# Grouped experts: gate and up products of the first 512 tokens moved into the router's stretch

## What is computed

```python
scores = jax.nn.sigmoid(h @ gate_w.T)                 # 32 experts
sc = scores + gate_bias
grp = sc.reshape(-1, G, E // G)                       # 8 groups of 4
gidx = top_k(top_k(grp, 2)[0].sum(-1), 4)[1]          # best 4 groups
masked = where(in_best_groups, sc, 0)
tki = top_k(masked, 8)[1]                             # best 8 experts
tkw = take(scores, tki); tkw = 2.5 * tkw / (tkw.sum(-1) + 1e-20)
combine = (one_hot(tki, E) * tkw[..., None]).sum(1)
g = silu(einsum('th,eih->tei', h, w_gate)); u = einsum('th,eih->tei', h, w_up)
routed = einsum('tei,ehi->th', g * u * combine[:, :, None], w_down)
shared = silu(h @ sh_gate.T) * (h @ sh_up.T) @ sh_down.T
x = x + layernorm(routed + shared)
```

## Time and profile before

| | |
|---|---|
| timed runs, median (lowest to highest) | 3097.4 us (3094.87 to 3097.8) |
| profiled execution, span | 3093.3 us |
| busy share: PE / DVE / ACT / POOL | 87% / 66% / 51% / 35% |
| last stage, first and last instruction of its engines | about 2849.7 to 3084.4 us |

### The profile page before, as it was taken

How to read it: one execution, slowest core, us unless ns; L and a number is a source line. 1 busy time by engine, 2 the same in 40 slices (tenths; PEclk the granted TensorE clock), 3 DMA queues, 4 the chain that set the end, 5 groups by cost and what they waited for, 6 DMA issues and landing times. The chain is left out here.

```text
span 3093.3 us, 55201 instructions
## 1 busy us (share of the span) xinstructions
PE 2694.2 (87%) x21256; PEld 1684.6 (54%) x21276; DVE 2049.2 (66%) x4308; ACT 1572.2 (51%) x3080; POOL 1072.5 (35%) x784
## 2 busy tenths in 40 slices
PE   8985899999799799999998888898877899777698
PEld 4552555566676566666666566465543334335465
DVE  5668999935644665546664665566439999996554
ACT  4334788852423444434554555366456676643122
POOL 3201000001243344434443553245226777773000
PEclk9995899989899899999999899998999999998899
DMA  1000000001120200000000000000013344340000
GB/s 55 1 4 1 2 3 3 3 2 82 33 89 22 84 1 1 1 1 1 1 1 1 29 1 1 1 1 1 1 66 129 137 144 144 136 143 21 1 1 14
DMA packets 34228, 105.41 MB, mean 34 GB/s; under 512 B 3456, under 2 KB 14592, under 8 KB 33200
## 3 DMA queue, kind: packets, MB, share of 16 engines
q1 hardware_dynamic: 31952, 97.69, 9.1%
q0 software_dynamic: 2016, 4.19, 0.4%
HBM read 94.01 MB, written 7.86 MB: 33 GB/s over the span
## 5 line engine op out<-in xcount | busy, mean ns | idle before, releaser
L2121 POOL TENSOR_TENSOR many_probs<-many_probs,many_rinv 128x2048 f32<-128x2048 f32 (+7 forms) x128 | 269.6, 2106 | 358.8 <-DVE many_rinv L2161 358.8
L1101 DVE TENSOR_REDUCE heads_halfmax<-heads_qmajor 128x1 f32<-128x512 f32 x512 | 316.3, 681 | 32.7 <-PE heads_qmajor L962 29.4
L3509 DVE TENSOR_TENSOR_SCAN stream_state<-stream_decay,stream_state 128x512 f32<-128x512 f32 x256 | 306.3, 1233 | 0.9 <-ACT stream_decay L3341 0.5
L1066 ACT ACTIVATE weights<-heads_kmajor 128x1024 f32<-128x1024 f32 x256 | 259.2, 1026 | 71.7 <-PE heads_kmajor L974 65.7
L2090 ACT ACTIVATE many_probs<-many_score,many_negmax 128x1024 f32<-128x1024 f32 (+7 forms) x256 | 187.4, 737 | 173.1 <-DVE many_negmax L2145 173.1
L2145 DVE TENSOR_REDUCE many_negmax<-many_score 128x1 f32<-128x1024 f32 (+7 forms) x256 | 184.4, 751 | 106.0 <-PE many_score L2019 104.3
L3179 PE MATMUL stream_yacc<-stream_state,ident 128*128 128x512 f32 x512 | 249.1, 614 | 0.4 <-POOL stream_state L3471 0.4
L3341 ACT ACTIVATE stream_decay<-weights,mamba_negA 128x512 f32<-128x512 f32 x256 | 173.0, 689 | 112.5 <-DVE stream_state L3509 111.3
L3471 POOL TENSOR_TENSOR stream_state<-XN,stream_state 128x1024 f32<-128x1024 f32 x85 | 200.2, 2359 | 81.6 <-DVE stream_state L3509 81.2
L2027 PE MATMUL many_ring<-ident,many_probs 128*128 128x128 f32 x1152 | 174.6, 279 | 23.4 <-POOL many_probs L2121 6.5
L3500 DVE TENSOR_TENSOR stream_state<-stream_bspread,stream_du 128x1024 f32<-128x1024 f32 x128 | 153.2, 1197 | 46.6 <-POOL stream_du L3447 38.6
(11 more groups left out here) (586 smaller groups left out, 5925.5 us busy)
## 6 DMA issues: line engine op xcount, KB each, us to landing
XN<-mamba_crows SPq DMA_DIRECT2D x85, 512.0 KB, 3.6
stream_crow<-mamba_crows SPq DMA_DIRECT2D x43, 512.0 KB, 3.7
weights<-in_w_dram SPq DMA_DIRECT2D x1, 6148.0 KB, 17.3
weights<-in_w_dram SPq DMA_DIRECT2D x1, 4274.0 KB, 12.9
weights<-in_w_dram SPq DMA_DIRECT2D x1, 3296.0 KB, 10.9
swiglu_pairs<-swiglu_fetched SPq DMA_DIRECT2D x1, 2310.0 KB, 10.4
weights<-in_w_dram SPq DMA_DIRECT2D x1, 2112.0 KB, 8.2
swiglu_fetched<-swiglu_pairs SPq DMA_DIRECT2D x4, 528.0 KB, 7.3
```

Of the source, the lines that this page charges most:

```text
L1066: nc.scalar.activation(probs_of(k).rearrange("p (a n) -> p a n", a=2), kmajor[:, at:at + 2, :], ACT.Exp, scale=SC).then_inc(exp_done, 1)
L1101: nc.vector.tensor_reduce(halfmax[:, g % 2, at, h % 2:h % 2 + 1], qmajor[:, (2 * n + j) % 3, :], AX, ALU.max).then_inc(max_done, 1)
L2121: nc.gpsimd.tensor_tensor(pair, pair, rinv[:, n % 4, :].unsqueeze(2).broadcast_to([P, 2, wide]), ALU.mult).then_inc(norm_done, 1)
L3509: nc.vector.tensor_tensor_scan(h[:, part(half)], decay[:, (2 * g + half) % DECAYS, :], h[:, part(half)], 0.0 if half == 0 else h[:, BANK - ...
```

## The change

Gate and up of the whole first block (`AHEAD` = 17 units) are issued on TensorE right after the router's matmuls, while VectorE runs the router. ScalarE takes the Silu of each into `ahead` and copies the up product from PSUM to `up_kept` (two buffers, so the copy waits for the product two units back). GpSimd multiplies the two in SBUF and leaves the result in `ahead`. The first half's transposes stand ahead of unit 15 on TensorE (`FIRST_TURN`), the second half's ahead of unit 16 (`SECOND_TURN`), and ScalarE's copies of them likewise. In the loop over all units TensorE then has only spread and down for units 0 to 16, and VectorE only the product with `spread`, with `ahead` as its second operand. From unit 17 on the loop is as before.

For the shared expert there is no spread any more. In the first block its down takes `ahead` directly, and in the others VectorE writes the product of up and Silu straight to `hidden`. So `wide_ones` is gone, and `hidden_at`, `unit_of`, `spread_at` and `unit_of_spread` turn unit numbers into counts of `hidden` and `spread` and back.

```diff
@@ -3570,6 +3570,20 @@
...
     UNITS = [(tc, c) for tc in range(NT // 4) for c in range(CH + 1)]
+    AHEAD = CH + 1
+    FIRST_TURN, SECOND_TURN = 15, 16
+
+    def hidden_at(n):
+        return n if n < CH else n - 1
+
+    def unit_of(h):
+        return h if h < CH else h + 1
+
+    def spread_at(n):
+        return n - n // (CH + 1)
+
+    def unit_of_spread(k):
+        return k + k // CH
     with Phase(nc, "grouped") as ph:
...
@@ -3586,8 +3600,9 @@
...
         select = ph.sb("select", [96, CH, P], BF16)
+        ahead = ph.sb("ahead", [P, AHEAD, BANK])
+        up_kept = ph.sb("up_kept", [P, 2, BANK])
         silu = ph.sb("silu", [P, 2, BANK])
-        wide_ones = ph.sb("wide_ones", [1, BANK])
         gated = ph.sb("gated", [P, 2, BANK])
...
@@ -3599,21 +3614,26 @@
...
                                 "sel_done"))
+        silu_ahead, up_ahead, ahead_done = ph.sem("silu_ahead"), ph.sem("up_ahead"), ph.sem("ahead_done")
         nz = Normaliser(nc, m, ph, "n_", True, False, EARLY[s])
...
         def _(pool):
-            nc.gpsimd.memset(wide_ones[:], 1.0).then_inc(sel_done, 1)
             nc.gpsimd.memset(select[:], 0.0).then_inc(sel_done, 1)
             for r in range(3):
-                pool.wait_ge(sel_done, r + 2)
+                pool.wait_ge(sel_done, r + 1)
 
...
                                         pattern=[[-2, CH], [-1, 2], [0, 64]], channel_multiplier=1).then_inc(sel_done, 1)
+            for n in range(AHEAD):
+                pool.wait_ge(silu_ahead, n + 1)
+                pool.wait_ge(up_ahead, n + 1)
+                nc.gpsimd.tensor_tensor(ahead[:, n, :], ahead[:, n, :], up_kept[:, n % 2, :],
+                                        ALU.mult).then_inc(ahead_done, 1)
             for q in EARLY[s]:
...
@@ -3628,45 +3648,57 @@
...
                 tc, c = UNITS[n]
-                if n >= 2:
-                    pe.wait_ge(gated_done, n - 1)
+                if 2 <= n < AHEAD + 2:
+                    pe.wait_ge(up_ahead, n - 1)
+                elif n >= AHEAD + 2:
+                    pe.wait_ge(gated_done, n - 1 - AHEAD)
                 for k in range(2):
...
                                      start=True, stop=True).then_inc(gu_done, 1)
-            gate_and_up(0)
-            gate_and_up(1)
-            pe.wait_ge(parts_done, 1)
-            for half in range(2):
-                if half:
-                    pe.wait_ge(turn_kept, 1)
+
+            def turn(half):
                 for j in range(8):
...
                 last.then_inc(turn_done, 1)
-            pe.wait_ge(turn_kept, 2)
-            pe.wait_ge(sel_done, 5)
+
+            for n in range(AHEAD):
+                if n == FIRST_TURN:
+                    pe.wait_ge(parts_done, 1)
+                    turn(0)
+                if n == SECOND_TURN:
+                    pe.wait_ge(turn_kept, 1)
+                    turn(1)
+                gate_and_up(n)
+            pe.wait_ge(sel_done, 4)
             for n in range(len(UNITS) + 1):
...
                     tc, c = UNITS[n]
-                    if n >= 2:
+                    if n >= AHEAD:
                         gate_and_up(n)
-                        pe.wait_ge(hid_done, n - 1)
                     if c < CH:
-                        nc.tensor.matmul(spread[:, n % 2, :], select[:, c, :], partsT[:, tc * BANK:(tc + 1) * BANK],
+                        if spread_at(n) >= 2:
+                            pe.wait_ge(hid_done, hidden_at(unit_of_spread(spread_at(n) - 2)) + 1)
+                        if c == 0 and tc == 2:
+                            pe.wait_ge(turn_kept, 2)
+                        nc.tensor.matmul(spread[:, spread_at(n) % 2, :], select[:, c, :],
+                                         partsT[:, tc * BANK:(tc + 1) * BANK],
                                          start=True, stop=True).then_inc(spread_done, 1)
-                    else:
-                        nc.tensor.matmul(spread[:, n % 2, :], m.ones[0:1, :], wide_ones[0:1, :], start=True,
-                                         stop=True).then_inc(spread_done, 1)
                 if n >= 1:
                     tc, c = UNITS[n - 1]
-                    pe.wait_ge(hid_done, n)
+                    if n - 1 == CH:
+                        pe.wait_ge(ahead_done, AHEAD)
+                        left = ahead[:, CH, :]
+                    else:
+                        pe.wait_ge(hid_done, hidden_at(n - 1) + 1)
+                        left = hidden[:, hidden_at(n - 1) % 3, :]
                     if c == 0 and tc > 0:
...
                         wt = shared_w[2] if c == CH else w["wd"][:, c * P:(c + 1) * P]
-                        last = nc.tensor.matmul(down[:, 0, j * P:(j + 1) * P], hidden[:, (n - 1) % 3, j * P:(j + 1) * P],
+                        last = nc.tensor.matmul(down[:, 0, j * P:(j + 1) * P], left[:, j * P:(j + 1) * P],
                                                 wt, start=(c == 0 and j == 0), stop=(c == CH), skip_group_check=True)
...
@@ -3674,16 +3706,28 @@
...
             nc.scalar.activation(scores[:].rearrange("p t e -> p (t e)"), spread[:, 0, :], ACT.Sigmoid).then_inc(sig_done, 1)
-            for half in range(2):
+            def keep_turn(half):
                 act.wait_ge(turn_done, half + 1)
...
                                      ACT.Copy).then_inc(turn_kept, 1)
-            for n in range(len(UNITS)):
+
+            for n in range(AHEAD):
+                if n == FIRST_TURN:
+                    keep_turn(0)
+                if n == SECOND_TURN:
+                    keep_turn(1)
                 act.wait_ge(gu_done, 2 * n + 1)
+                nc.scalar.activation(ahead[:, n, :], gate_up[:, 2 * (n % 2), :], ACT.Silu).then_inc(silu_ahead, 1)
+                act.wait_ge(gu_done, 2 * n + 2)
                 if n >= 2:
-                    act.wait_ge(gated_done, n - 1)
+                    act.wait_ge(ahead_done, n - 1)
+                nc.scalar.activation(up_kept[:, n % 2, :], gate_up[:, 2 * (n % 2) + 1, :], ACT.Copy).then_inc(up_ahead, 1)
+            for n in range(AHEAD, len(UNITS)):
+                act.wait_ge(gu_done, 2 * n + 1)
+                if n >= AHEAD + 2:
+                    act.wait_ge(gated_done, n - 1 - AHEAD)
                 nc.scalar.activation(silu[:, n % 2, :], gate_up[:, 2 * (n % 2), :], ACT.Silu).then_inc(silu_done, 1)
-                if UNITS[n][1] == 7 and UNITS[n][0] >= 1:
+                if UNITS[n][1] == 7:
                     nz.scale(act, 0, UNITS[n][0] - 1)
...
@@ -3741,16 +3785,30 @@
...
                 if n < len(UNITS):
-                    dve.wait_ge(silu_done, n + 1)
-                    dve.wait_ge(gu_done, 2 * n + 2)
-                    nc.vector.tensor_tensor(gated[:, n % 2, :], gate_up[:, 2 * (n % 2) + 1, :], silu[:, n % 2, :],
-                                            ALU.mult).then_inc(gated_done, 1)
-                    dve.wait_ge(gated_done, n + 1)
-                    dve.wait_ge(spread_done, n + 1)
-                    if n >= 3:
-                        dve.wait_ge(down_done, n - 2)
-                    nc.vector.tensor_tensor(hidden[:, n % 3, :], spread[:, n % 2, :], gated[:, n % 2, :],
-                                            ALU.mult).then_inc(hid_done, 1)
+                    h = hidden_at(n)
+                    shared = UNITS[n][1] == CH
+                    if n >= AHEAD:
+                        dve.wait_ge(silu_done, n + 1 - AHEAD)
+                        dve.wait_ge(gu_done, 2 * n + 2)
+                        if shared:
+                            dve.wait_ge(down_done, unit_of(h - 3) + 1)
+                        into = hidden[:, h % 3, :] if shared else gated[:, n % 2, :]
+                        product = nc.vector.tensor_tensor(into, gate_up[:, 2 * (n % 2) + 1, :], silu[:, n % 2, :], ALU.mult)
+                        product.then_inc(gated_done, 1)
+                        if shared:
+                            dve.wait_ge(gated_done, n + 1 - AHEAD)
+                            dve.sem_inc(hid_done, 1)
+                        else:
+                            dve.wait_ge(gated_done, n + 1 - AHEAD)
+                    elif not shared:
+                        dve.wait_ge(ahead_done, n + 1)
+                    if not shared:
+                        dve.wait_ge(spread_done, spread_at(n) + 1)
+                        if h >= 3:
+                            dve.wait_ge(down_done, unit_of(h - 3) + 1)
+                        left = ahead[:, n, :] if n < AHEAD else gated[:, n % 2, :]
+                        nc.vector.tensor_tensor(hidden[:, h % 3, :], spread[:, spread_at(n) % 2, :], left,
+                                                ALU.mult).then_inc(hid_done, 1)
                 if n >= 1 and UNITS[n - 1][1] == CH:
...
                     dve.wait_ge(down_done, n)
```

## The result

| | before | changed |
|---|---|---|
| median (lowest to highest) | 3097.6 us (3094.87 to 3099.36) | 3071.5 us (3070.43 to 3073.03) |
| profiled execution, span | 3093.3 us | 3068.7 us |
| first gate and up to the last copy of `Y` (VectorE) | 228.2 us | 203.7 us |
| first gate and up to unit 17's | 79.65 us | 58.68 us |

The ratio is 0.9913, 95% interval 0.9901 to 0.9925: 26.1 us less. 3077.0 was forecast, with 3064 to 3087 as the range. The forecast gain was 20.4 us, the spans differ by 24.6.

What follows compares the result with a forecast made beforehand. TensorE was taken as the bound in the loop, idle while VectorE ran the router. Gains of 17.3 us up to unit 17 and 3.15 from the ones make 20.4: 3097.4 - 20.4 = 3077.0 us, range 3064 to 3087.

Steps and rivals of the forecast that it cites:

- A: The forecast as summed: products hold some router steps, two steps pass per unit; 3077.0 us, own range 3071 to 3083, chance 0.60.
- Step 1: TensorE during the router: gate and up of fifteen units fill the idle hole, ending at 2882.8.
- Step 2: ScalarE: Silu and Copy at 0.60 each take 1.20 of each unit's 1.72 us, so hidden; table load costs nothing.
- rival E: ScalarE: Silu and Copy need different tables, each switch costs 1.28 us, the move gives nothing; about 3094.6, chance 0.05.
- Step 3: GpSimd: 17 products at 1.27 us of each unit's 1.72 keep up as a queue.
- Rival D: GpSimd: products themselves stretch while taking turns with VectorE, at 2.54 us each the kernel is slower; 3104.2, chance 0.04.
- Step 4: Router on VectorE: products hold two-input steps, two steps per unit; late by 9.0 us in all, parts ready at 2890.2.
- B: Router on VectorE: nothing is held up, parts ready at 2879.4 before TensorE asks; 3065.0, chance 0.15.
- C: Router on VectorE: every product stands in its way in full, fifteen products, parts ready at 2898.4; 3085.2, chance 0.16.
- Step 4, the low clock: TensorE after waiting for the router: clock falls, two sets of transposes and two units take 9 us, ending at 2899.3.
- Step 5: Loop over units 0 to 16, only spread and down: 1.3 plus 17.3 us, unit 17 at 2917.9, 17.3 us gained.
- Step 6: Shared expert: no spread of ones in three further shared units, 1.05 each, gains 3.15 us.

Runs made afterwards that it cites:

- experiment 1: The changed kernel without GpSimd's seventeen products, GpSimd only counting them off (output misses the up factor in the first block): 3065.4 us, ratio 0.9899.
- experiment 2: The changed kernel with each product replaced by a GpSimd memset of 1360 columns, which writes SBUF and reads nothing: 3065.5 us, ratio 0.9892.
- experiment 3: The changed kernel with each product replaced by a one-input GpSimd copy of 1250 columns, SBUF to SBUF: 3072.2 us, ratio 0.9916.
- experiment 4: The changed kernel, computing in full, with each two-input router step reading one operand from PSUM: 3065.2 us, and 3062.5 us when run again.
- Experiment 6: The kernel before with only the shared expert's part: no ones, no spread for it, product straight to `hidden`: 3091.9 us, ratio 0.9983.
- experiment 7: The changed kernel with GpSimd products of 256 columns instead of 512: 3069.4 us, ratio 0.9907.

## Why the prediction was right, and where it was off

The mechanism and the likeliest case (A) held; the gain was underestimated, 20.4 for 24.5 us in the stage. By its steps:

- **Step 1, fifteen units in the hole.** 2882.8 was forecast, 2882.9 it is.
- **Step 2, ScalarE hides.** One table load, at 2856.30, and a Copy of 0.60 us. Right; so rival E is out.
- **Step 3, GpSimd keeps up at 1.27 us.** The shortest products take 1.26, the first fifteen 1.31 on average. Rival D, stretched products, is out.
- **Step 4, the router is held.** Right in kind. By stretch: late by 3.6 (forecast 3.6), then 6.8 (forecast 7.7), then 7.95 at the transposes (forecast 9.0). Two steps per unit is what the trace shows: every second one is held, by one product each. The second stretch was 1 us too dear because of what was counted. Its ninth step, the cast, has one SBUF input and took 0.20 us, not half a unit (0.86); and the reduction of 0.69, added in full, ran beside a product that held the next step only for the rest of its time (0.56 us instead of 0.40). In the third stretch the held step adds 0.9 us and the addition of a constant, which the prediction left out, 0.2: 1.2 together, where 1.3 was put. Rivals B (nothing held) and C (every product in full) would have put the transposes at 2882.8 and 2898; they start at 2889.2. Experiments 1 to 4 show the cause.
- **Step 4, the low clock: the term that was mis-sized.** Two sets of transposes and two units were put at 9.0 us, all at the low level; they took 6.07 (2889.19 to 2895.26). I had taken the 10.5 us of rows 2 for how long the low level lasts after TensorE resumes. But there TensorE was busy 5.91 of 10.5 us: it waited between its pieces for 1.11, 1.11 and 2.32 us (rows below). From the end of the last wait, at 2889.00, it worked on without a pause, and from 2892.5 on the clock was high. In the changed kernel no such wait follows 2889.19, and the clock is high from 2892.5 on as well: unit 16 runs at full rate. The same happens in its second execution and in experiment 3. The waits would explain the difference in these executions, but no run changed them alone, so that is read from the rows and not shown by an experiment. This is 2.9 of the 4.1 us.
- **Step 5, the loop.** 18.6 us forecast, 18.9 it takes (2895.26 to 2914.15). Units follow at 1.11 us and the first down waits, as summed.
- **Step 6, the ones.** 3.15 forecast; from unit 17 to the last copy of `Y` it is 3.5 less (148.53 and 145.04). Experiment 6 shows the missing part: 1.24 instead of 1.05 per unit.

The rows for the clock: TensorE's waits and two windows in the kernel before, then a window of the changed kernel (columns as in rows 2).

```profile
2883.44 1.09 PE L3645 MATMUL grouped_turned<-identb,grouped_parts 128*96 128x128 bf16 x8 [1.11 <-ACT grouped_partsT L3679]
2885.64 1.03 PE L3657 MATMUL grouped_spread<-grouped_partsT,grouped_select 96*128 96x512 bf16 x2 [1.11 <-ACT grouped_partsT L3679]
2889.00 2.07 PE L3669 MATMUL grouped_down<-weights,grouped_hidden 128*128 128x128 f32 x8 [2.32 <-DVE grouped_hidden L3752]
...
2889.00:2892.50 3.50, 3.50 (x10) 2.54 (x11) 1.23 (x2) 0.00 (x0) 0.00 (x0) 0.50 0.02 5
2892.50:2895.00 2.50, 2.50 (x14) 1.59 (x13) 1.26 (x2) 0.60 (x1) 0.00 (x0) 0.99 0.00 0
...
2892.50:2895.00 2.50, 2.50 (x14) 1.29 (x13) 0.00 (x0) 1.98 (x4) 1.02 (x1) 1.00 0.00 0
```

Together: 1.0 from the router, 2.9 from the clock, 0.35 from the ones, less 0.3 in the loop make 4.0 of the 4.1 us. The medians differ by 1.6 us more than the stage does. That is within the interval (23 to 31 us for the gain). And the 4.1 us that I put around the span set a median against the span of one execution: the changed kernel's profiled execution took 3070.5 us around a span of 3068.7, 1.8 more. That slip does not enter the forecast, which takes a gain off the median. All the terms but the loop's erred to the same side; none of them hid another.

## What to carry to other kernels

When work is moved into a stretch where another engine is the bound, ask what the moved work does to that engine. Here the hole in TensorE was 20.6 us, but the products that came with the move, on GpSimd, made the router 8 us longer. TensorE lost 6.4 us waiting for it and 1.6 us more to the clock. If a chain on VectorE must run beside GpSimd, put one operand of each two-input step into PSUM where a bank is free: here it made steps longer by some 1.5 us (one more of 0.69, three casts at 0.69 instead of 0.43) and gave back 7.8 us of the stage. Measure such edits from start to start within the stage; the scatter of the stages ahead (5 us here) hides them in the total.

## What the runs showed of the hardware

- A GpSimd instruction that reads SBUF, with one input or two, holds VectorE steps with two SBUF inputs to its end (0.292 us becomes 0.751 with the copies and 0.770 with the products, on average over four), and is itself held by one that came first (1.27 to 1.43 us). The Trainium skill says so in "SBUF — State Buffer", section "Who interferes with whom", and the trace agrees in every row of the router. Rows 9 do not: a GpSimd root of 1.05 us on four columns, which reads SBUF too, starts during the first of four such additions, and the four take 0.89 us, unheld. No run here tells why.
- A GpSimd instruction that only writes SBUF doesn't hold those, but holds VectorE's casts and constant additions from SBUF to SBUF: 0.43 to 0.95 us and 0.17 to 1.30. The same section of the Trainium skill names casts and additions of a constant (`tensor_scalar`) among the instructions that can enter a mode of VectorE which contends with GpSimd, and experiment 2 agrees. With the cast's source in PSUM (experiment 4) it takes 0.69 us, and no hold is seen.
- TensorE's clock fell to the low level with a wait of only 2.62 us (experiment 7): unit 15 took 3.21 us, where it takes 1.77 in experiment 1. In the kernel before it was still at 1.00 for the first 3.6 us of the long wait (rows 2), and experiment 2's wait of 0.65 us passed without a fall. So the 3.6 us of rows 2, by which the prediction judged the pause, is no safe length.
